# Third phase of a four-phase transformer kernel: TensorE lays the by-key mask ahead of its wait for the by-query slot

## What is computed

```python
def _L3_xattn_ref(values, keys, queries, mask, w_out, b_out):
    ...                                   # 16 heads of 16
    energy = jnp.einsum('nqhd,nkhd->nhqk', q, k)
    energy = jnp.where(mask == 0, jnp.float32(-1e+20), energy)
    attn = jax.nn.softmax(energy / math.sqrt(EMBED), axis=3)
    out = jnp.einsum('nhql,nlhd->nqhd', attn, v).reshape(N, q_len, HEADS * HEAD_DIM)
    return out @ w_out.T + b_out
```

## Time and profile before

| | us |
|---|---|
| median of three runs | 4302.57 |
| span of the profiled execution, first to last instruction | 4135.2 |
| outside this span (median less span) | 167.4 |
| TensorE busy (matmul) | 3911.6 |
| VectorE busy | 2263.8 |
| ScalarE busy | 1747.7 |
| first and last mask matmul (L2331) | 2985.8 and 3634.7 |

### The profile page before, as it was taken

One profiled execution on the slowest core, in us unless ns is written; L12 is line 12 of the kernel. 1 busy time (PEld: TensorE's weight loads), 2 busy tenths in 40 slices (PEclk: granted clock), 3 DMA queues, 4 the chain that ended last, 5 costly groups with the idle time before them and its releaser, 6 DMA issues. The chain is left out here.

```text
span 4135.2 us, 77612 instructions
## 1 busy us (share of the span) xinstructions
PE 3911.6 (95%) x28960; PEld 2760.0 (67%) x28960; DVE 2263.8 (55%) x6853; ACT 1747.7 (42%) x3685; POOL 1067.4 (26%) x1239
## 2 busy tenths in 40 slices
PE   7999999999999999999998989999899999889998
PEld 4666666666666666666665549997666666459965
DVE  4556555655565565556555542123677777544445
ACT  4455545554544555455455221111354454414420
POOL 2222221222222122212221001111112232245667
PEclk9999999999999999999999999999999999999999
DMA  3003113303321330233031027995112221139954
GB/s 119 1 14 120 59 65 118 120 11 110 120 84 40 118 120 28 94 120 110 17 113 62 26 78 273 330 334 204 29 58 72 78 88 50 54 136 332 337 180 150
DMA packets 285453, 472.85 MB, mean 114 GB/s; under 512 B 23008, under 2 KB 224608, under 8 KB 276512
## 3 DMA queue, kind: packets, MB, share of 16 engines
q1 hardware_dynamic: 227632, 371.88, 26.4%
q0 software_dynamic: 24480, 66.88, 5.3%
q10 hardware_dynamic: 32976, 29.13, 2.0%
HBM read 266.74 MB, written 201.06 MB: 113 GB/s over the span
## 5 line engine op out<-in xcount | busy, mean ns | idle before, releaser
L488 POOL TENSOR_SCALAR a_wide_p<-a_wide_p,a_w_inv 128x512 f32<-128x512 f32 x512 | 355.3, 706 | 1427.5 <-DVE a_w_inv L1149 1427.5
L923 ACT ACTIVATE a_wide_p<-a_wide_p,a_row_min 128x512 f32<-128x512 f32 x512 | 363.6, 713 | 143.5 <-DVE a_row_min L1144 143.4
L1219 DVE TENSOR_REDUCE a_q_pad<-ring 128x4 f32<-128x1024 f32 x256 | 301.0, 1218 | 76.7 <-PE ring L712 76.7
L1144 DVE CUSTOM_DVE_ANT_0 a_wide_p<-ring,a_neg_keys 128x512 f32<-128x512 f32 x387 | 256.4, 688 | 135.8 <-PE ring L572 135.7
L572 PE MATMUL ring<-a_qk 64*128 64x512 f32 x774 | 288.3, 642 | 10.7 <-DVE a_wide_pt L1154 4.0
L980 ACT ACTIVATE a_probs<-ring 128x1024 f32<-128x1024 f32 x256 | 250.6, 1019 | 72.7 <-PE ring L726 72.7
L1669 PE MATMUL ring<-b_xgt,b_we 128*128 128x128 f32 x2016 | 235.6, 275 | 0.8 <-DVE b_xgt L1859 0.5
L2783 DVE CUSTOM_DVE_ANT_0 shared_w<-ring,c_neg_mask 128x256 f32<-128x256 f32 x512 | 186.5, 421 | 90.8 <-PE ring L2346 90.8
L1669 PEld LDWEIGHTS ring<-b_xgt,b_we 128*128 128x128 f32 x2016 | 230.2, 192 | 1.3 <-DVE b_xgt L1859 0.7
L2592 ACT ACTIVATE c_probs<-ring 128x1024 f32<-128x1024 f32 x128 | 130.9, 1023 | 177.5 <-PE ring L2338 177.4
L551 PE MATMUL acc<-a_kv_t,shared_w 128*128 128x512 f32 x392 | 191.5, 611 | 1.2 <-ACT a_kv_t L914 1.2
(11 more groups left out here) (456 smaller groups left out, 8600.0 us busy)
## 6 DMA issues: line engine op xcount, KB each, us to landing
d_cells<-a_neg_keys SPq DMA_DIRECT2D x66, 2048.0 KB, 16.5
b_we<-in_experts SPq DMA_DIRECT2D x63, 1536.0 KB, 9.0
d_we<-in_experts SPq DMA_DIRECT2D x159, 256.0 KB
d_results<-d_yb ACTq DMA_DIRECT2D x159, 128.0 KB
a_k_t<-in_ctx_keys SPq DMA_DIRECT2D x16, 512.0 KB
a_v_pad<-in_ctx_values SPq DMA_DIRECT2D x16, 512.0 KB
c_k_t<-in_ctx_keys SPq DMA_DIRECT2D x16, 512.0 KB, 3.8
c_v_pad<-in_ctx_values SPq DMA_DIRECT2D x16, 512.0 KB, 3.6
```

The lines of the kernel that those rows point to most:

```text
L488: ins = pool.tensor_scalar(wide_p[:, h % 4, t, :], wide_p[:, h % 4, t, :], w_inv[:, t, h:h + 1], 1.0, ALU.mult, ALU.mult)
L923: ins = act.activation(wide_p[:, h % 4, t, :], wide_p[:, h % 4, t, :], ACT.Exp, scale=-1.0, bias=row_min[:, h, t:t + 1], accum_out=row_sum ...
L1144: dve.tensor_tensor_reduce(wide_p[:, h % 4, t, :], wbank(name), neg_keys[w % 2][:], -0.125, 3.0e38, ALU.add, ALU.min, row_min[:, h, t:t + ...
L1219: dve.tensor_reduce(q_pad[:, :, 2 * i:2 * i + 2, HD].rearrange("p t h -> p h t"), s, AX.X, ALU.max, negate=True).then_inc(nr.taken(name), 1)
```

## The change

In `n_scores` the block for the by-query part, with its waits (keys and turned queries at call 0, the `sr` slot at each call), is moved behind the block for the by-key part, which has the `tr` wait and the two mask matmuls. All other text stays.

```diff
                         def n_scores(qb, s, tb, i):
-                            if qb is not None:
-                                if s == 0:
-                                    pe.wait_ge(keys_loaded[qb % 3], 16 * (qb // 3 + 1))
-                                    sr.wait_taken(pe, ("Q", qb))
-                                sr.wait_room(pe, ("S", qb, s))
                             if tb is not None:
                                 if i == 0:
                                     tr.wait_taken(pe, ("Q2", tb))
                                 tr.wait_room(pe, ("T", tb, i))
                                 for j in range(2):
                                     pe.matmul(tbank[:, 512 * j:512 * j + 512], ident_bf[:], neg_mask_t[:].rearrange("p k n -> p (k n)"),
                                               start=True, stop=False, skip_group_check=True)
+                            if qb is not None:
+                                if s == 0:
+                                    pe.wait_ge(keys_loaded[qb % 3], 16 * (qb // 3 + 1))
+                                    sr.wait_taken(pe, ("Q", qb))
+                                sr.wait_room(pe, ("S", qb, s))
                             for m in range(2):
                                 for j in range(2):
```

## The result

The changed kernel takes 4275.99 us (median of five runs, 4271.54 to 4284.84) against 4302.57 for the kernel before (five runs, 4301.93 to 4311.85): ratio 0.9939, 95% interval 0.9926 to 0.9951. The forecast was 4278.5, a gain of 24.1 us; measured are 26.6, with the interval 21 to 32. The time was right, but one step behind it was wrong, and the first line of the new profile shows it.

What follows compares the result with a forecast made beforehand. TensorE was taken to pace the third phase; stalls at the mask, 13.6 + 3.4 + 7.1 us, summed to 24.1, so 4302.6 - 24.1 = 4278.5 us, range 4269 to 4290.

Steps and rivals of the forecast that it cites:

- What bounds the stage: Third phase: TensorE paces each batch, busy 41.81 of 43.40 us, with about 1.6 us of real holes.
- No cost of the order or of the wait: Between mask and scores: TensorE's instruction order stays, and a satisfied wait there costs 0.
- Call 4, 0.50 us, limited by the by-key slot: Call 4 stood 1.17 us; ScalarE's exponential frees the by-key slot only 0.50 us before VectorE's last maximum ends; gain 0.50.
- Calls 1 and 7, 0.53 and 0.33: Regular batch: call 1 gains the mask's full 0.53 us, call 7 the 0.33 us by which TensorE was early.
- 0.24 is taken off: Call 1: 0.24 of TensorE's 0.83 us earliness is no hole, as an earlier matmul still streams; 0.59 remain.
- The sum over the phase: 54 stalls: ten regular batches 13.6 us, first two 3.4, last three 7.1; together 24.1 us, all on the path.
- 167.4 us lie around the span and stay: Whole kernel: median time 4302.57 less profiled span 4135.2 us was taken as time outside the span, unchanged.
- The clock as a spread of 5 us: Range's lower end, 4269: the upper-bound gain of 28.6 us and 5 us for clock dips removed or brought.
- rival 2: The moved wait costs one exposed weights load, 0.19 us in each of 105 calls: 4298.5, no change; chance 4%.
- rival 3: The wait is taken only after the mask streamed out, hand-over paid twice, 0.42 us in 105 calls: 4322.6; chance 3%.
- rival 4: At the mask the by-key slot is the late one, so nothing moves: 4302.6; chance 1%.
- rival 1: Part of the gain returns as other waits, at calls 4 to 6; 14.6 us remain, 4288; chance 8%.

Runs made afterwards that it cites:

- run 5: Kernel before, with the already satisfied wait for the by-query slot asked a second time between mask and scores: ratio 1.0009.
- run 4: Kernel before with the swap at calls 2, 3, 5 and 6 only: 4135.82 us against 4139.00, ratio 0.9992.
- run 2: The changed kernel again, on the same chip as an unchanged control of the kernel before: 4113.95 us, ratio 0.9940.
- run 7: Kernel before, without the swap, with the transposes L2269 moved from behind call 4 to ahead of it: ratio 0.9994.
- run 1: The kernel before, unchanged, as a control: 4140.21 us against 4139.46, ratio 0.9999.

## Why the prediction was right, and where it was not

- **What bounds the stage**: right. TensorE paces it; of the 1.3 us by which the batch shortened 1.1 are holes closed, and neither VectorE's nor ScalarE's work changed.
- **No cost of the order or of the wait**: right (runs 5 and 4).
- **Call 4, 0.50 us, limited by the by-key slot**: right, 0.50, with the mask waiting for the exponential.
- **Calls 1 and 7, 0.53 and 0.33**: mis-sized, 0.40 and 0.39. At call 1 the term "0.24 is taken off" came from a mask behind 256-column matmuls of full width. Behind L2284 the load is late by 0.41 us of "issue", and about 0.4 should have been taken off. At call 7 the mask's load now starts 0.16 us before the previous group has ended (3174.12 against 3174.28), which the stalled one could not. The two nearly cancel: 1.31 for 1.36.
- **The sum over the phase**: 24.1 forecast. Two spans at nearly the same clock give 24.1 (4135.2 less 4111.1), those of one chip 34.0; the three comparisons of the swap with before give 26.6, 25.5 and 31.6 us, each with an interval that holds 24.1. By periods, batches 1 and 2 gave 2.8 (forecast 3.4) and the ten regular ones 13.1 (13.6), so 8.2 (7.1) are left. From the start of the last regular batch to the last mask's load the profiles of before and of run 2 differ by 10.0 us (3457.62 to 3634.59, 3442.41 to 3609.34); 8.7 of them belong to the last three batches. There the kernel before spent 3.4 us more at the lower level, worth 1.7 by the same estimate, so about 7.0 stand against the 7.1. The pieces without the clock give 22.9 where 24.1 were forecast: the terms were near, call by call, and that the spans gave 24.1 exactly is luck.
- **"167.4 us lie around the span and stay"**: wrong. Every execution with both numbers on record has its time 1.6 to 2.9 us above its span; the rest was the difference between the profiled execution and the timed runs, which were of another speed. It did no harm, since the gain is 0.6% of either time, but a change whose work stood in stretches at the lower level would have been priced wrongly. That the median lay so far above the span should have been named as a question.
- **The clock as a spread of 5 us**: too small as a description. The kernel before takes 137 to 163 us longer on some chips than on others; the forecast range held the time because before and after were timed on the same chip.
- **Rivals**: 2 and 3 excluded by run 5, 4 by the gain itself. Of rival 1, waits that come back elsewhere, the swap shows next to nothing (0.66 at call 4 is the rest of the old hole), but the edit of run 7 shows it: of the 0.6 us filled in, 0.23 came off the batch.
- **The row reading that every mask with both slots free starts its load before the previous one ended**: true of 26 of the 66 such loads of the kernel before; the other 40 start 0.02 to 0.12 us after. The conclusion, that a satisfied wait costs nothing, stands on runs 4 and 5.

## What to carry to other kernels

Where an engine waits for two slots and has work that needs only one of them, ask for that one first: each stall gives back the least of the work's length, the engine's earliness, and the lead of the one slot over the other. List the stalls one by one before summing: three of seven calls carried all of a regular batch's gain here. And fill holes of a pair of engines together: a filling ahead of one wait gave half as much while the mask still stood behind the next one.

## What the runs showed of the hardware

- The same program takes 4139 us on two of the chips, 4276 and 4300 on two others, and 4303 in the first measurement. The mean granted clock is 0.99 on the former and 0.97 to 0.98 on the latter (in the first measurement, that of the changed kernel's runs). On the latter it fell once in nearly every batch of this stage from about 3131 us on; on the former never between 3000 and 3539. Why was not tried.
- The recorded clock explains only about half of the difference. Between the first profile of the changed kernel and that of run 2 the spans differ by 163 us (4274.1 and 4111.1). The lost clock is 0.028 of the one and 0.010 of the other, 120 and 41 us, so it accounts for about 79, an estimate from these numbers. In the batches looked at, the rest is a hold of TensorE of about 3.7 us that begins before the clock's fall.
- A satisfied wait ahead of a weights load costs nothing that can be measured here (at most 0.07 us each), where the load couldn't start earlier anyway.
- After matmuls of 32 rows the next load of another form starts 0.33 or 0.34 us after the last one, and after those of 32 columns the next one of full width 0.41 or 0.42, in every regular batch of runs 1 and 2's kernels. Between groups of full width that wait for nothing it starts between 0.31 us before and 0.11 us after the last one's end.
